# Weighted source one-hots in one operation, one column of each pair on VectorE and the other on GpSimd

## The chip, the cores and the metric

The kernel runs on one core of one Trainium2 chip. The metric is the device time of one execution in microseconds (us). The engines have the profile's names: PE is TensorE (matmuls), PEld its weight loads, DVE is VectorE, ACT is ScalarE, POOL is GpSimd, SP is SyncE.

## The reference, cut to what matters

Two layers of a graph network with attention and feed-forward parts work on 1250 nodes with 512 features. Only the edges of the graph convolution bear on this case:

```python
def _L0_gnn_ref(x, edge_index, edge_attr, W, b):
    ...
    deg = jax.ops.segment_sum(ew, col_f, num_segments=n)
    dinv = jnp.where(deg > 0, jax.lax.rsqrt(deg), 0.0)
    norm = dinv[row_f] * ew * dinv[col_f]
    h = x @ W
    msg = h[row_f] * norm[:, None]
    out = jax.ops.segment_sum(msg, col_f, num_segments=n)
    return out + b
```

There are 21250 edges, sorted by destination, each with a source, a destination and a weight.

## The kernel before

The kernel doesn't gather rows. It builds the dense matrix `AT` (source by destination, 10 x 10 tiles of 128) from the edges, and both graph layers then multiply by it. The edges lie in `CH` = 170 columns of 128, two columns to a pair, `CP` = 85 pairs. A pair's destinations lie in a window of `WIN` = 20 nodes. For pair `g`, TensorE multiplies a left one-hot `Loh` (128 edges by the 128 values of the source's low bits, times the edge's weight) with a right one-hot `Roh` (128 edges by 200 keys, which are 10 source tiles by 20 places in the window). The weight is kept as two parts, `whl`, a rounded one and the rest, so each pair has two columns times two parts: four matmuls of 128x200, all added in one PSUM bank `pW[g % 2]`. VectorE then adds the bank to the window of `AT`.

Who makes what for a pair, before the change:

- VectorE (`onehots`, L1327): two plain one-hots of the source, 128x128, into `onehot`; then the right one-hot of column 1 (L1329). It reports `oh_src` and `oh_dve`.
- GpSimd (L1000): one product of 128x512 that takes the two plain one-hots times the two weight parts into `Loh`. It waits for `oh_src` and reports `oh_pool`.
- ScalarE (L564, L566): the right one-hot of column 0, in two steps. It reports `oh_act`.
- TensorE (`adj`, L1989): waits for `oh_dve`, `oh_act`, `oh_pool` and, from the third pair on, for `a_acc`, the addition two pairs back. It reports `a_mm`.
- VectorE (`pairs_upto`, L1358): waits for `a_mm`, adds the bank to `AT`, and goes on with the one-hots three pairs further on.

`Loh` has `SLOTS` = 4 slots and `Roh` `RSLOTS` = 3, and `slot_free` is the wait for a slot: VectorE and ScalarE begin pair `g` when TensorE has done pair `g` - 3.

The pairs are woven into the products of the layer. A product (`product`, L2005) multiplies a tile of 128 nodes by one of the four weight matrices, in four blocks of three matmuls of 128x512. A fixed table (`pairs_by`, with `ADJ0` = 28 and `ADJ1` = 132) puts the 85 pairs behind the blocks 28 to 132, so that most blocks are followed by a pair. Between these come `kv` (L2034, twelve small matmuls) and the transposes of the next tile (L1976). For each tile VectorE also has `k_elu`, `xt_lo`, `v_lo` and `q_elu`, one operation of 128x512 each, and GpSimd has `k_lo` (L985, writes `khl`) once for 12 or 13 pairs. Every engine has one queue in the order in which the code is written.

Five operations of GpSimd elsewhere in the program serve as prices below: L1131 (a multiplication and an addition, both with a pointer, that is one value for each partition), L1115 (a multiplication and an addition of constants), L1117 and L1110 (a lone compare with a constant), and L1159 (a lone multiplication by a constant). Two of VectorE differ in a pointer: L1506 has one, L1862 a constant in its place.

When the pairs are done, VectorE reduces `AT` to the degrees (L1425), which TensorE's further work needs. SyncE loads `raw` after the last pair into the region that `onehot` shares.

Of the kernel before, what the change touches and what calls it, by code (L numbers as in the profile page):

```python
# [21 lines left out]
F32 = mybir.dt.float32  # L22
F32R = mybir.dt.float32r
I32 = mybir.dt.int32
ALU = mybir.AluOpType
# [3 lines left out]
P = 128  # L29
# [18 lines left out]
SLOTS = 4  # L48
ZERO_POOL, ZERO_DVE, ZERO_ACT = ((0, 1), (5, 6, 7)), (2, 3, 4), (8, 9)
RSLOTS = 3  # L50
# [52 lines left out]
def build(nc, a, out):  # L103
    ctx = ExitStack()
    with ctx:
# [24 lines left out]
        def region(name, *groups):  # L130
# [3 lines left out]
            for group in groups:  # L134
                used = 0
                with ExitStack() as r:
# [28 lines left out]
        srclo, key, whl, iota_src, iota_key = (RE[n] for n in ("srclo", "key", "whl", "iota_src", "iota_key"))  # L165
# [25 lines left out]
        R1 = region("hold_raw",  # L191
                    [("erow", [P, 3, 2, P], I32), ("frow", [P, 4, 2, P], F32)],

                    [("edge", [P, 3, CH]), ("egap", [P, 2 * D - 3 * CH]), ("away", [P, 2, T * WIN]), ("eq", [P, D])],
                    [("onehot", [P, SLOTS, 2, P], F32R)],
                    [("raw", [P, KC, D], F32)],
                    [("xb", [P, 2, D]), ("brow", [P, 2, D])],
                    [("vraw", [P, D]), ("b2", [P, 2, D], F32R)])
        erow, frow, edge, raw, xb, brow = (R1[n] for n in ("erow", "frow", "edge", "raw", "xb", "brow"))
        away, eq, onehot_ = R1["away"], R1["eq"], R1["onehot"]  # L200
        vraw, b2 = (R1[n] for n in ("vraw", "b2"))

        R2 = region("hold_weights",
# [35 lines left out]
        khl, vhl, Loh, Roh, ATs, Wv, qx, shl = (R3[n] for n in ("khl", "vhl", "Loh", "Roh", "ATs", "Wv", "qx", "shl"))  # L239
# [74 lines left out]
        S = {}  # L314
# [56 lines left out]

            return 8 * min(t, LAG) + 16 * max(0, t - LAG) + 4 * k

        def slot_free(eng, g):

            if g >= RSLOTS:
                eng.wait_ge(S["a_mm"], g - RSLOTS + 1)

        def evicted(w, t):

# [577 lines left out]
        def _(pool):  # L958
# [35 lines left out]

            pool.wait_ge(S["e_dve"], 1)
            for g in range(CP):
                pool.wait_ge(S["oh_src"], g + 1)
                w = whl[:, 2 * g:2 * g + 2, :].bitcast(F32).rearrange("p c (k n) -> p c k n", n=1).broadcast_to([P, 2, 2, P])
                o = onehot_[:, g % SLOTS].bitcast(F32).rearrange("p c (k n) -> p c k n", k=1).broadcast_to([P, 2, 2, P])
                pool.tensor_tensor(Loh[:, g % SLOTS], o, w, ALU.mult).then_inc(S["oh_pool"], 1)  # L1000
                for t in range(LAG, T):
                    if g == min(CP - 1, pairs_by(block_of(t, 2)) + 2):
                        k_lo(t)
# [22 lines left out]
            k = [0]  # L1026
# [66 lines left out]
            n = t1 - t0  # L1093
# [109 lines left out]
        def _(v):  # L1203
# [119 lines left out]

            def onehots(g):
                slot_free(v, g)
                for c in range(2):
                    ins = v.tensor_scalar(onehot_[:, g % SLOTS, c, :], iota_src[:], srclo[:, 2 * g + c:2 * g + c + 1], None, ALU.is_equal)  # L1327
                ins.then_inc(S["oh_src"], 1)
                v.tensor_scalar(Roh[:, g % RSLOTS, 1, :], iota_key[:], key[:, 2 * g + 1:2 * g + 2], None,  # L1329
                                ALU.is_equal).then_inc(S["oh_dve"], 1)  # L1330
# [635 lines left out]
        def _(pe):  # L1966
# [14 lines left out]
            def adj(g):  # L1981
                pe.wait_ge(S["oh_dve"], g + 1)
                pe.wait_ge(S["oh_act"], g + 1)
                pe.wait_ge(S["oh_pool"], g + 1)
                if g >= 2:
                    pe.wait_ge(S["a_acc"], g - 1)
                for c in range(2):
                    for part in range(2):
                        ins = pe.matmul(pW[g % 2][:, 0:T * WIN], Loh[:, g % SLOTS, c, part, :], Roh[:, g % RSLOTS, c, :],  # L1989
                                        start=(c + part == 0), stop=(c + part == 2))  # L1990
                ins.then_inc(S["a_mm"], 1)
# [612 lines left out]
```

## Time and profile before

| | |
|---|---|
| Median of 3 executions | 609.44 us (607.0 to 612.33) |
| The profiled execution | 611.55 us |
| Its span in the profile | 609.8 us |
| Busy: PE / PEld | 566.8 us (93%) / 457.4 us (75%) |
| Busy: DVE / ACT / POOL | 470.9 us (77%) / 331.7 us (54%) / 257.7 us (42%) |
| The stage with the pairs | 45.14 to 187.66 us |

The span is the time between the first and the last record of the profile; the 1.75 us between it and the execution's own time lie around it. Busy times are the union of an engine's records. TensorE's matmuls are pipelined and their ends are modelled, so a start to the next start says more there than a duration. The stage runs from the transposes behind the count of outside edges to the end of the last pair's matmuls.

### The profile page before, as it was taken

To read this page: it belongs to the slowest core of one execution; us is meant where nothing else is said; L and a number is where in the kernel's file an instruction comes from. 1 tells how busy PE (TensorE), PEld (TensorE's weight loads), DVE (VectorE), ACT (ScalarE), POOL (GpSimd) and SP (SyncE) were. 2 spreads that over 40 slices of the span, in tenths; PEclk is the share of its full clock that TensorE was granted. 3 is DMA by queue.
4 is the path that set the end of the run, shared out by engine and by line. 5 is a ranking of instruction groups with operands and counts; after the bars stand their busy time and mean duration, and the time that the engine had idled before them with its cause. 6 is when DMAs were issued, how large, how long until landed. Compare 5 with 4: busy or idle time off the path is not lost.

```text
span 609.8 us, 8679 instructions
## 1 busy us (share of the span) xinstructions
PE 566.8 (93%) x2933; PEld 457.4 (75%) x2933; DVE 470.9 (77%) x1043; ACT 331.7 (54%) x620; POOL 257.7 (42%) x290
## 2 busy tenths in 40 slices
PE   2998989988999999999999989999999999998977
PEld 2776877776887787888886757788878878687867
DVE  7679988979999688667988786778676556478865
ACT  7767868767775562213135656545456773423172
POOL 3647767667778515544833880005011221031020
PEclk9999989999999999999999999999999998899969
DMA  9300000000002021013113010000002000020004
GB/s 321 139 2 0 2 1 2 1 1 2 1 1 70 2 69 35 18 34 81 31 43 105 2 69 1 0 1 2 0 13 76 0 1 2 12 76 0 1 18 152
DMA packets 15046, 21.11 MB, mean 35 GB/s; under 512 B 3261, under 2 KB 6001, under 8 KB 15003
## 3 DMA queue, kind: packets, MB, share of 16 engines
q1 hardware_dynamic: 13674, 17.94, 9.2%
q10 hardware_dynamic: 1328, 2.62, 1.2%
q8 instruction: 24, 0.39, 0.3%
q14 instruction: 20, 0.16, 0.1%
HBM read 18.00 MB, written 2.56 MB: 34 GB/s over the span
## 4 chain that ended last, share of the span: by engine, by line
PE 62%; DVE 22%; ACT 7%; issue 5%; POOL 2%; DVEq 1%; ACTq 0%; POOLq 0%
PE p L2154 8%; PE p L1989 4%; PE pQ L2274 4%; PE p L2274 4%; PE pQ L2005 3%; DVE onehot L1327 3%; PE p L2410 2%; PE pH L2166 2%; PE pH L2005 2%; DVE p L1425 2%; PE p L2239 2%; PE pQ L2166 2%; PE pKV L2239 2%; POOL Loh L1000 2%; PE p L2005 2%
## 5 line engine op out<-in xcount | busy, mean ns | idle before, releaser
L1000 POOL TENSOR_TENSOR Loh<-onehot,whl 128x512 fp32r<-128x512 f32 x85 | 89.5, 1053 | 48.3 <-DVE onehot L1327 48.3
L1327 DVE TENSOR_SCALAR onehot<-iota_src,srclo 128x128 fp32r<-128x128 f32 x170 | 74.7, 479 | 0.7 <-DVE flagint L1339 0.7
L1989 PEld LDWEIGHTS p<-Roh,Loh 128*128 128x128 f32 x340 | 48.4, 192 | 31.1 <-issue 27.0
L2154 PE MATMUL p<-G,ATs 128*128 128x512 f32 x300 | 70.5, 391 | 0.0
L2154 PEld LDWEIGHTS p<-G,ATs 128*128 128x128 f32 x300 | 55.9, 188 | 11.6 <-issue 0.2
L1989 PE MATMUL p<-Roh,Loh 128*128 128x200 f32 x340 | 53.7, 281 | 11.3 <-POOL Loh L1000 4.8
L564 ACT ACTIVATE away<-iota_key,key 128x200 f32<-128x200 f32 x85 | 38.7, 456 | 24.4 <-PE p L1989 24.4
L2005 PE MATMUL pQ<-wsl,xT 128*128 128x512 f32 x168 | 48.4, 418 | 2.4 <-DVE xT L1241 2.4
L2005 PE MATMUL pH<-wsl,xT 128*128 128x512 f32 x168 | 46.4, 404 | 0.0
L1358 DVE TENSOR_TENSOR AT<-AT,p 128x200 f32 x85 | 30.1, 354 | 14.0 <-PE p L1989 8.8
L566 ACT ACTIVATE Roh<-away,onesf 128x200 fp32r<-128x200 f32 x85 | 39.4, 463 | 2.8
L1173 POOL TENSOR_TENSOR xT<-xn,xT 128x512 fp32r<-128x512 f32 x10 | 12.9, 1292 | 63.6 <-ACT xT L809 60.7
L1018 POOL TENSOR_TENSOR ATs<-AT,ATs 128x1280 fp32r<-128x1280 f32 x10 | 29.9, 2992 | 18.6 <-ACT ATs L624 18.3
L2005 PEld LDWEIGHTS pQ<-wsl,xT 128*128 128x128 f32 x168 | 30.6, 199 | 8.0 <-DVE xT L1241 3.2
L663 ACT ACTIVATE xT<-pT 128x512 fp32r<-128x512 f32 x10 | 6.0, 598 | 53.2 <-PE pT L2141 53.2
L2005 PE MATMUL p<-wsl,xT 128*128 128x512 f32 x120 | 33.2, 399 | 0.0
L2005 PEld LDWEIGHTS pH<-wsl,xT 128*128 128x128 f32 x168 | 29.7, 192 | 4.4
L2274 PE MATMUL p<-Wk,xT 128*128 128x512 f32 x120 | 30.1, 398 | 0.9 <-ACT rt L770 0.9
L2274 PE MATMUL pQ<-Wq,xT 128*128 128x512 f32 x120 | 29.9, 397 | 0.7 <-DVE xT L1668 0.5
L1329 DVE TENSOR_SCALAR Roh<-iota_key,key 128x200 fp32r<-128x200 f32 x85 | 26.6, 313 | 0.0
L1198 POOL TENSOR_SCALAR nodes<-nodes,small,nmr 128x512 f32<-128x512 f32 x10 | 8.0, 811 | 43.2 <-DVE sn L1881 43.2
L2274 PEld LDWEIGHTS pQ<-Wq,xT 128*128 128x128 f32 x120 | 21.9, 188 | 5.4 <-DVE xT L1668 0.6
(648 smaller groups left out, 1432.2 us busy)
## 6 DMA issues: line engine op xcount, KB each, us to landing
xb<-in_x SPq DMA_DIRECT2D x9, 256.0 KB, 2.6
out<-nodes SPq DMA_DIRECT2D x9, 256.0 KB
wraw<-in_L_mix_w_qkv ACTq DMA_DIRECT2D x2, 1024.0 KB, 7.5
raw<-in_L_mix_w_qkv SPq DMA_DIRECT2D x2, 1024.0 KB, 5.0
nodes<-in_x SPq DMA_DIRECT2D x1, 1024.0 KB, 9.0
wraw<-in_L_mix_w_qkv SPq DMA_DIRECT2D x1, 1024.0 KB, 11.3
wraw<-in_L_gnn_W SPq DMA_DIRECT2D x1, 1024.0 KB, 13.5
raw<-in_L_mix_w_out SPq DMA_DIRECT2D x1, 1024.0 KB, 5.3
```

The lines of the kernel that those rows point to most:

```text
L564: act.activation(away[:, g % 2, :], iota_key[:], ACT.Abs, bias=key[:, 2 * g:2 * g + 1], scale=-1.0).then_inc(S["oh_y"], 1)
L566: act.activation(Roh[:, g % RSLOTS, 0, :], away[:, g % 2, :], ACT.Relu, bias=onesf[:, 0:1], scale=-1.0).then_inc(S["oh_act"], 1)
L1000: pool.tensor_tensor(Loh[:, g % SLOTS], o, w, ALU.mult).then_inc(S["oh_pool"], 1)
L1018: pool.tensor_tensor(ATs[:, t % 2, 1], AT[:, :, t * P:(t + 1) * P], ATs[:, t % 2, 0].bitcast(F32), ALU.subtract).then_inc(S["ats_lo"], 1)
L1327: ins = v.tensor_scalar(onehot_[:, g % SLOTS, c, :], iota_src[:], srclo[:, 2 * g + c:2 * g + c + 1], None, ALU.is_equal)
L1329: v.tensor_scalar(Roh[:, g % RSLOTS, 1, :], iota_key[:], key[:, 2 * g + 1:2 * g + 2], None, ALU.is_equal).then_inc(S["oh_dve"], 1)
L1358: v.tensor_tensor(win, win, pW[g % 2][:, 0:T * WIN].rearrange("p (s w) -> p s w", s=T), ALU.add)\
L1989: ins = pe.matmul(pW[g % 2][:, 0:T * WIN], Loh[:, g % SLOTS, c, part, :], Roh[:, g % RSLOTS, c, :], start=(c + part == 0), stop=(c + part ...
L2005: ins = pe.matmul(bank[:, :], xT[:, t % XR, x, c, :], wsl[:, w, y, c, :], start=(c == 0 and n == 0), stop=(c == KC - 1 and n == 2))
L2154: ins = pe.matmul(pG[u][:, :], ATs[:, u, x, s_, :], G[:, y, s_, :], start=(s_ + n == 0), stop=(s_ == T - 1 and n == 2))
L2166: ins = pe.matmul(pM[u][:, :], xT[:, QT[u], x, c, :], WO[:, y, c, :], start=(c + n == 0), stop=(c == KC - 1 and n == 2))
L2274: ins = pe.matmul(o, xT[:, QT[u], x, c, :], w[:, y, c, :], start=(c + n == 0), stop=(c == KC - 1 and n == 2))
```

## The change

Each left one-hot is now made with its weight in it, by one `tensor_scalar` with two operations: compare `iota_src` with the source, multiply by the weight's part. VectorE makes the two parts of column 0, GpSimd the two parts of column 1, both straight into `Loh`. The buffer `onehot` is gone. GpSimd no longer waits for VectorE; it waits for its slot by itself, at the depth of `SLOTS` = 4. TensorE waits for `oh_src` too, besides `oh_pool`.

```diff
-        def slot_free(eng, g):
-
-            if g >= RSLOTS:
-                eng.wait_ge(S["a_mm"], g - RSLOTS + 1)
+        def slot_free(eng, g, slots=RSLOTS):
+
+            if g >= slots:
+                eng.wait_ge(S["a_mm"], g - slots + 1)
+
+        def weighted(eng, g, c, part):
+
+            col = slice(2 * g + c, 2 * g + c + 1)
+            return eng.tensor_scalar(Loh[:, g % SLOTS, c, part, :], iota_src[:], srclo[:, col], whl[:, col, part].bitcast(F32), ALU.is_equal, ALU.mult)
...
             pool.wait_ge(S["e_dve"], 1)
             for g in range(CP):
-                pool.wait_ge(S["oh_src"], g + 1)
-                w = whl[:, 2 * g:2 * g + 2, :].bitcast(F32).rearrange("p c (k n) -> p c k n", n=1).broadcast_to([P, 2, 2, P])
-                o = onehot_[:, g % SLOTS].bitcast(F32).rearrange("p c (k n) -> p c k n", k=1).broadcast_to([P, 2, 2, P])
-                pool.tensor_tensor(Loh[:, g % SLOTS], o, w, ALU.mult).then_inc(S["oh_pool"], 1)
+                slot_free(pool, g, SLOTS)
+                for part in range(2):
+                    ins = weighted(pool, g, 1, part)
+                ins.then_inc(S["oh_pool"], 1)
...
             def onehots(g):
                 slot_free(v, g)
-                for c in range(2):
-                    ins = v.tensor_scalar(onehot_[:, g % SLOTS, c, :], iota_src[:], srclo[:, 2 * g + c:2 * g + c + 1], None, ALU.is_equal)
+                for part in range(2):
+                    ins = weighted(v, g, 0, part)
                 ins.then_inc(S["oh_src"], 1)
...
             def adj(g):
                 pe.wait_ge(S["oh_dve"], g + 1)
                 pe.wait_ge(S["oh_act"], g + 1)
+                pe.wait_ge(S["oh_src"], g + 1)
                 pe.wait_ge(S["oh_pool"], g + 1)
```

In GpSimd's queue the start of the pairs reads before, from the last of the splits of the weights on (`wsl`) through the first `khl`:

```order
L980 TENSOR_TENSOR wsl<-wraw,wsl 128x512 x3
L1000 TENSOR_TENSOR Loh<-onehot,whl 128x512 [waits oh_src,e_dve]
L1000 TENSOR_TENSOR Loh<-onehot,whl 128x512 [waits oh_src] x5
L985 TENSOR_TENSOR khl<-rt,khl 128x512 [waits k_hi]
L1000 TENSOR_TENSOR Loh<-onehot,whl 128x512 [waits oh_src] x13
```

and now:

```order
L984 TENSOR_TENSOR wsl<-wraw,wsl 128x512 x3
L381 TENSOR_SCALAR Loh<-iota_src,srclo,whl 128x128 [waits e_dve]
L381 TENSOR_SCALAR Loh<-iota_src,srclo,whl 128x128 x7
L381 TENSOR_SCALAR Loh<-iota_src,srclo,whl 128x128 [waits a_mm]
L381 TENSOR_SCALAR Loh<-iota_src,srclo,whl 128x128
L381 TENSOR_SCALAR Loh<-iota_src,srclo,whl 128x128 [waits a_mm]
L381 TENSOR_SCALAR Loh<-iota_src,srclo,whl 128x128
L989 TENSOR_TENSOR khl<-rt,khl 128x512 [waits k_hi]
```

The first four pairs (eight operations) wait for nothing but the edges' weights and keys, and from the fifth on each pair waits for TensorE's count of done pairs in place of VectorE's one-hots; `khl` stands behind the sixth pair in both.

In TensorE's queue a block, its pair and the next block read before:

```order
L2005 MATMUL pQ<-wsl,xT 128x512 x2
L1989 MATMUL p<-Roh,Loh 128x200 [waits oh_pool,a_acc,oh_act,oh_dve]
L1989 MATMUL p<-Roh,Loh 128x200 x3
L2005 MATMUL pQ<-wsl,xT 128x512 [waits w_lo]
L2005 MATMUL pQ<-wsl,xT 128x512 x2
```

and now:

```order
L2010 MATMUL pQ<-wsl,xT 128x512 x2
L1994 MATMUL p<-Roh,Loh 128x200 [waits oh_pool,oh_src,a_acc,oh_act,oh_dve]
L1994 MATMUL p<-Roh,Loh 128x200 x3
L2010 MATMUL pQ<-wsl,xT 128x512 [waits w_lo]
L2010 MATMUL pQ<-wsl,xT 128x512 x2
```

Nothing has moved there but the one wait that is added to the pair's first matmul.

## Rows read from the trace of the kernel before

**Rows 1.** Windows: span, busy us and instructions of PE, PEld, DVE, ACT, POOL; PEclk; DMA
```profile
45.14:187.66 142.52, 131.22 (x749) 105.23 (x750) 128.06 (x365) 104.25 (x223) 98.68 (x93) 0.99 0.00 1
65.00:70.00 5.00, 5.00 (x33) 4.45 (x33) 4.49 (x14) 4.50 (x10) 3.67 (x4) 1.00 0.01 2
120.00:125.00 5.00, 4.24 (x24) 3.14 (x23) 5.00 (x13) 3.87 (x9) 4.03 (x5) 1.00 0.00 0
```

**Rows 2.** PE in order of time, 61 to 68 us: start us, us, operation
```profile
61.64 1.47 PE L2034 MATMUL pKV<-vhl,khl 128*128 128x130 f32 x12
62.95 0.91 PE L2005 MATMUL pH<-wsl,xT 128*128 128x512 f32 x3
...
66.41 0.87 PE L2005 MATMUL pH<-wsl,xT 128*128 128x512 f32 x3
67.12 0.59 PE L1989 MATMUL p<-Roh,Loh 128*128 128x200 f32 x4
67.55 0.60 PE L1976 MATMUL pT<-ident,xn 128*128 128x128 f32 x4
67.91 0.48 PE L2005 MATMUL p<-wsl,xT 128*128 128x512 f32 x1
```

**Rows 3.** Waits of PE in the stage: us in total, times, longest us
```profile
PE p L1989 <- POOL Loh L1000: 4.8, 11, 0.9
PE p L1989 <- DVE AT L1358: 4.1, 5, 1.7
```

**Rows 4.** DVE, then POOL and PE in order of time, 117 to 121 us, DVE at 137
```profile
117.33 0.47 DVE L1327 TENSOR_SCALAR onehot<-iota_src,srclo 128x128 fp32r<-128x128 f32 x2
117.72 0.31 DVE L1329 TENSOR_SCALAR Roh<-iota_key,key 128x200 fp32r<-128x200 f32 x1
117.95 0.35 DVE L1358 TENSOR_TENSOR AT<-AT,p 128x200 f32 x1
118.22 0.98 DVE L1327 TENSOR_SCALAR onehot<-iota_src,srclo 128x128 fp32r<-128x128 f32 x2
...
119.63 2.04 DVE L1327 TENSOR_SCALAR onehot<-iota_src,srclo 128x128 fp32r<-128x128 f32 x2
...
117.88 1.05 POOL L1000 TENSOR_TENSOR Loh<-onehot,whl 128x512 fp32r<-128x512 f32 x1 [1.04 <-DVE onehot L1327]
119.29 1.05 POOL L1000 TENSOR_TENSOR Loh<-onehot,whl 128x512 fp32r<-128x512 f32 x1 [0.36 <-DVE onehot L1327]
120.30 1.29 POOL L985 TENSOR_TENSOR khl<-rt,khl 128x512 fp32r<-128x512 f32 x1
...
119.21 0.67 PE L1989 MATMUL p<-Roh,Loh 128*128 128x200 f32 x4 [0.28 <-POOL Loh L1000]
...
137.12 0.36 DVE L1358 TENSOR_TENSOR AT<-AT,p 128x200 f32 x1 [3.38 <-issue]
```

**Rows 5.** The page's costliest groups: busy us, mean ns of one | idle before
```profile
L1327 DVE TENSOR_SCALAR onehot<-iota_src,srclo 128x128 fp32r<-128x128 f32 x170 | 74.7, 479 | 0.7 <-DVE flagint L1339 0.7
```

**Rows 6.** Groups by line of POOL's TENSOR_SCALAR: busy us, mean ns | idle before
```profile
L1131 POOL TENSOR_SCALAR nodes<-nodes,small,nmr 128x512 f32<-128x512 f32 x10 | 7.5, 765 | 0.1
L1115 POOL TENSOR_SCALAR first<-first 128x16 f32<-128x16 f32 x1 | 0.2, 205 | 3.2 <-DVE first L1682 3.2
L1117 POOL TENSOR_SCALAR XB<-first 128x16 f32<-128x16 f32 x1 | 0.3, 252 | 0.1
L1110 POOL TENSOR_SCALAR XB<-XB 128x256 f32<-128x256 f32 x1 | 0.9, 857 | 0.1
L1159 POOL TENSOR_SCALAR pairq<-pairs 128x64 fp32r<-128x64 f32 x1 | 0.4, 408 | 0.0
```

**Rows 7.** Groups by line of DVE: one form with a pointer, one with a constant
```profile
L1506 DVE SCALAR_TENSOR_TENSOR nodes<-p,dinv,nodes 128x512 f32<-128x512 f32 x10 | 7.5, 751 | 0.9 <-PE p L2154 0.6
L1862 DVE SCALAR_TENSOR_TENSOR nodes<-p,nodes 128x512 f32<-128x512 f32 x10 | 6.8, 681 | 0.0
```

**Rows 8.** The chain that ended last, behind the last pair: start us, us
```profile
188.96 11.87 DVE p L1425
```

More of the change, by code:

```diff
@@ L194, in build @@
                     [("edge", [P, 3, CH]), ("egap", [P, 2 * D - 3 * CH]), ("away", [P, 2, T * WIN]), ("eq", [P, D])],
-                    [("onehot", [P, SLOTS, 2, P], F32R)],
                     [("raw", [P, KC, D], F32)],
@@ L199, in build @@
         erow, frow, edge, raw, xb, brow = (R1[n] for n in ("erow", "frow", "edge", "raw", "xb", "brow"))
-        away, eq, onehot_ = R1["away"], R1["eq"], R1["onehot"]
+        away, eq = R1["away"], R1["eq"]
         vraw, b2 = (R1[n] for n in ("vraw", "b2"))
```

## The prediction

> **What bounds the kernel now.** I read the stretches first, then TensorE's order of time at a good and a bad place, then the order of time of the engines that feed it, and last the waits. The change touches one stage: the 85 pairs run from 45.14 us, where TensorE has finished the count of outside edges, to 187.66 us, the end of the last pair. In that stage TensorE is busy for 131.22 of 142.52 us [rows 1], which looks like a full engine. It isn't. Between 65 and 70 us it issued 33 matmuls, between 120 and 125 us only 24, in both at a granted clock of 1.00 [rows 1]; its records stretch when it has to wait. The good place gives the price of everything on TensorE, start to start: a pair's four matmuls 67.12 to 67.55 = 0.43 us, a block of three products 66.41 to 67.12 = 0.71, the twelve of kv 61.64 to 62.95 = 1.31, the four transposes 67.55 to 67.91 = 0.36 [rows 2]. The stage holds 85 pairs, 104 blocks, six kv and six groups of transposes: 36.6 + 73.8 + 7.9 + 2.2 = 120.4 us. So TensorE loses 22 us to its feeders. Its plain waits (4.8 us on GpSimd's product, 4.1 on the addition to AT) show less than half of that [rows 3].
>
> The feeders run in a ring. At 117 to 122 us the reader sees two one-hots on VectorE, 0.47 us for both when GpSimd is idle, 0.98 us when GpSimd's product is in the air: the second pair starts at 118.22 and ends at 119.20, which is 0.27 after GpSimd's 117.88 + 1.05 = 118.93. Then GpSimd starts at 119.29, 0.09 later, and holds VectorE's next pair in turn. Product to product, 117.88 to 119.29, is 1.41 us [rows 4]. TensorE in the same place could take a pair every 0.43 + 0.71 = 1.14 us, so this ring sets the pace wherever each block has its pair. The total says that this is the rule: the one-hots kept VectorE busy for 74.7 us, where 85 pairs at 0.47 would be 40, so some 35 us of that is being held [rows 4, 5]. With khl in GpSimd's queue VectorE's two one-hots ran 2.04 us in place of 0.98 (119.63) [rows 4], so the ring takes 1.06 more, seven times. 85 × 1.41 + 7 × 1.06 = 127 us of the 142.5; the other 15 are the first pairs, stalls of VectorE like the 3.38 us with no releaser shown at 137 us [rows 4], and places in which TensorE itself was late.
>
> **The change on GpSimd.** 85 products of 1.05 us go [rows 4], and 170 compares with a multiplication, 128x128, come. No row shows that operation. Its nearest rows are in two families [rows 6]. Multiplication and addition with two pointers, 128x512, took 765 ns, and two such with constants on 128x16 took 205: 0.190 us and 1.12 ns for each element, so 0.33 us for 128. A lone compare took 252 ns on 16 elements and 857 on 256: 0.212 us and 2.52 ns, so 0.53 us; a lone multiplication, 408 ns on 64, is on that dear line or above it. So what is cheap is the joined multiplication and addition, not two operations as such. If each operation paid the dear rate by itself it would be 0.212 + 2 × 128 × 0.00252 = 0.86 us. I take 0.56, the compare's line, which is the nearest operation, with 0.03 for the second; bounds 0.33 and 0.86. For a pair: 1.12 us, from 0.66 to 1.72, against 1.05 before, but without VectorE ahead of it. GpSimd now waits for the pair four back on TensorE, and may do the first four while it used to wait at the start.
>
> **The change on VectorE.** Two plain one-hots a pair become two with a second pointer. A pointer cost 751 - 681 = 70 ns on a comparable form [rows 7]; between 0 and 0.07 each, so 0 to 0.14 a pair. I take 0.05 for both, since one pointer is already being read. VectorE's own work in a pair is 0.27 (addition to the next one-hot, 117.95 to 118.22) + 0.39 (117.33 to 117.72) + 0.23 (117.72 to 117.95) = 0.89 us [rows 4], now 0.94 to 1.03.
>
> **How they share.** VectorE's compares stand still while GpSimd works. But the two held one-hots ended 0.27 us after GpSimd, of which the second took its usual 0.19, so the first needed only 0.08 more. And when GpSimd went from the product straight to khl (119.29 + 1.05, then 120.30), one of VectorE's two got through between and only the second was held; khl took 1.29 all the same [rows 4]. So one compare slips in at each handover, at no cost to GpSimd. Let p be GpSimd's operation. I count from the end of a pair's last feeder on VectorE, Roh. TensorE's pair follows and is reported about 1.0 us later (an estimate: 0.43 of matmuls, and what lay between GpSimd's end at 118.93 and the start at 119.21 of TensorE's pair, twice [rows 2, 4]); there GpSimd starts its two operations, for the pair four on. Those of the cycle before ended at 1.0 + 2p - C. VectorE has one one-hot through at their handover, ends the other 0.08 after their end, and Roh with 0.28 behind it; that is the end of the next Roh, so C = 1.0 + 2p - C + 0.36, or C = 0.68 + p. At p = 0.56 that is 1.24 us a pair, against 1.41. It can't be under GpSimd's own 2p + 0.1 (1.22) or VectorE's 0.94.
>
> The feeders then need 85 × 1.24 + 7 × 1.06 = 113 us, under TensorE's 120.4. TensorE becomes the bound on average, though not in stretches with a pair behind every block (1.24 against 1.14), where a lead of three pairs covers some of it. What stays: VectorE's stalls with no releaser (3.38 at 137; this one left TensorE short by 1.2), the first pairs (some 2 us), k_elu and xt_lo of 1.2 us in a row on VectorE. I put these at 11 to 13 us: 120.4 + 12 = 132.5, so the stage gives back **10 us**.
>
> The Trainium skill (SBUF — State Buffer, Who interferes with whom) says that the pair of ports is locked for the whole instruction, whoever comes first, and the other fully blocks. That speaks against this change. By the recorded durations it would make 0.47 + 0.31 + 1.05 = 1.83 us a pair before, and 0.78 + 1.12 = 1.90 after, a loss of 6 us in 85. The trace agrees that the loser is held, but not with the sum: the ring took 1.41.
>
> **Edits with one answer.** The onehot buffer isn't needed; no transfer waits for it. TensorE's new wait for oh_src stands in a queue that ran into a pair 0.43 us behind the last block with four waits already, so I cost it at nothing; if each showed, 85 × 0.05 = 4 us. The seven khl on GpSimd come two to three pairs earlier in the order of time, and may wait for ScalarE; behind them only pairs four ahead are queued. After the stage the path is VectorE's reduction of 11.9 us [rows 8], which starts at the last addition, and nothing earlier holds it. So all that the stage gives reaches the end.
>
> **The sum.** 611.55 us (span 609.8, 1.75 around it) - 10 = 601.5 for that execution, which lay 2.1 over the median of 609.44. Against the median: 599.5, said as 600.
>
> **Rivals.**
> (1) GpSimd on the cheap line, p = 0.33. C falls to 1.01, TensorE is the bound nearly throughout and the stage takes 120.4 + 6 us: 16 us gained, 594. For it: the two-pointer row of 765 ns. Against: every compare in the trace is dear. The Trainium skill (GPSIMD Engine Reference, Performance pitfalls for Q7 kernels) gives a compare-and-select body 1.03 to 2.03 cycles an element, which at its 1.2 GHz is an estimate of 0.9 to 1.7 ns and would bring this rival's time; the compare's 2.52 ns doesn't agree [rows 6].
> (2) **Slower: GpSimd becomes the bound.** With both operations at the dear rate, p = 0.86 and C = 2p + 0.1 = 1.82: 85 × 1.82 + 7.4 = 162 us, and 5 for the start, 167 against 142.5: 634. It decides above the point where 85 × (2p + 0.1) eats what the ring had, 127 - 7.4 = 120: p = 0.66. Half way, at 0.76, C = 1.62 and the time is 618 to 625. For it: the lone multiplication at 408 ns on 64 elements shows how dear one step is. Against: one operation or two need not double the loop.
> (3) The compares slip in less than I think, and VectorE is held for all of GpSimd's 1.12: C = 0.27 + 1.12 = 1.39 and more with what used to hide under the product (0.6 us of evictions four times in 12 pairs). Then 606 to 612, no change.
> (4) The change may not do all it says: without its fast form the one-hot on VectorE takes 0.07 us longer but isn't held. That ends near the forecast.
>
> **Chances.** Forecast (596 to 603): 0.40, case 4 in it. Rival 1: 0.18. Rival 3 with p near 0.66: 0.19. Rival 2: 0.23. Two executions of this kernel differ by up to 0.9% (607.0 to 612.33), so 1%, or 6 us, is what a measurement can tell from no change. Faster takes rival 1 and nearly all of the forecast: 0.57; within 1%: 0.20; slower: 0.23. The range runs from 592, under rival 1, to 630, where about half of rival 2 is in it; some 0.14 stay out.
>
> **What the profile after would show.** The 170 operations on GpSimd at 0.50 to 0.62 us; above 0.7, rival 2, with TensorE waiting for GpSimd in most pairs. VectorE's 170 weighted one-hots with a mean between 0.3 and 0.45 us, where it is 0.479 now [rows 5]. 30 or more matmuls in most 5 us of the stage. No wait of GpSimd for VectorE; its idle time now ends with TensorE's pairs. The last pair near 178 us, the reduction right behind it, and the rest of the program as long as before (422 us). Wrong would be an end of the stage outside 170 to 185, or a gain there that is lost again after it.

## The result and the profile after

| | before | after |
|---|---|---|
| Median (six executions each, same chip) | 607.1 us (605.62 to 612.33) | 620.01 us (618.63 to 621.53) |
| Profiled execution, its span | 611.55, 609.8 | 620.04, 618.3 |
| End of the last pair | 187.66 us | 196.73 us |
| Start of the reduction behind it | 188.96 us | 198.02 us |

The change made the kernel slower by 2.0%: the ratio is 1.0196, with a 95% interval from 1.016 to 1.0232. (This ratio and those below aren't quotients of the two medians.) The profiled executions differ by 8.5 us only, since the one of before lay 4.5 above this median (the last section shows where such 4 us come from). I read the page first: the busy times, the chain by engine, and the three groups that answer to [rows 5] and to GpSimd's new operation (busy us, mean ns | idle before).

```profile
span 618.3 us, 8765 instructions
...
PE 565.1 (91%) x2933; PEld 453.1 (73%) x2933; DVE 458.8 (74%) x1043; ACT 332.6 (54%) x620; POOL 314.3 (51%) x375
...
PE 50%; POOL 24%; DVE 17%; ACT 7%; issue 2%; ACTq 0%; DVEq 0%
...
L381 POOL TENSOR_SCALAR Loh<-iota_src,srclo,whl 128x128 fp32r<-128x128 f32 x170 | 145.9, 872 | 1.2 <-PE p L1994 1.2
...
L1362 DVE TENSOR_TENSOR AT<-AT,p 128x200 f32 x85 | 30.3, 356 | 35.6 <-PE p L1994 28.7
L381 DVE TENSOR_SCALAR Loh<-iota_src,srclo,whl 128x128 fp32r<-128x128 f32 x170 | 55.7, 380 | 0.7 <-DVE flagint L1343 0.7
```

One row settles what bounds the stage. GpSimd's 170 operations took 145.9 us with 1.2 us of idle time between them: the engine never had to wait for anybody. VectorE, which the old ring held, has lost that: its 170 compares take 55.7 us in place of 74.7 [rows 5], and it waits 28.7 us for TensorE before the addition. Before, GpSimd had 48.3 us of idle time in front of its products, all of it waiting for VectorE:

```profile
L1000 POOL TENSOR_TENSOR Loh<-onehot,whl 128x512 fp32r<-128x512 f32 x85 | 89.5, 1053 | 48.3 <-DVE onehot L1327 48.3
```

The windows say the same; they are the whole stage, the 5 us that [rows 1] shows of before, and the rest of the program (span, busy us and instructions of PE, PEld, DVE, ACT, POOL; PEclk; DMA).

```profile
45.00:196.73 151.73, 131.73 (x749) 103.12 (x750) 115.65 (x365) 105.09 (x223) 150.11 (x172) 1.00 0.00 1
120.00:125.00 5.00, 4.25 (x23) 3.01 (x22) 4.53 (x12) 3.62 (x8) 5.00 (x6) 1.00 0.00 0
196.73:618.30 421.57, 401.63 (x2037) 324.96 (x2036) 309.54 (x602) 194.50 (x351) 135.94 (x167) 0.98 0.11 33
```

GpSimd is busy for 150.11 of 151.73 us, where it was 98.68 of 142.52 [rows 1]. TensorE issues 23 matmuls from 120 to 125 us, one less than before. The rest takes 421.6 us against 422.1, so the end of the stage, 9.1 us later, accounts for all of the 8.5 us that the profiled execution lost. In order of time, the stretch that [rows 4] shows of before reads (start us, us, operation, idle before):

```profile
116.81 6.13 POOL L381 TENSOR_SCALAR Loh<-iota_src,srclo,whl 128x128 fp32r<-128x128 f32 x7
...
117.85 0.67 PE L1994 MATMUL p<-Roh,Loh 128*128 128x200 f32 x4 [0.40 <-ACT Roh L570]
...
118.93 0.60 DVE L381 TENSOR_SCALAR Loh<-iota_src,srclo,whl 128x128 fp32r<-128x128 f32 x2
119.44 0.32 DVE L1333 TENSOR_SCALAR Roh<-iota_key,key 128x200 fp32r<-128x200 f32 x1
119.66 0.67 PE L1994 MATMUL p<-Roh,Loh 128*128 128x200 f32 x4 [0.45 <-DVE Loh L381]
...
121.37 0.66 PE L1994 MATMUL p<-Roh,Loh 128*128 128x200 f32 x4 [0.33 <-DVE Loh L381]
...
122.91 1.32 POOL L989 TENSOR_TENSOR khl<-rt,khl 128x512 fp32r<-128x512 f32 x1
123.00 1.34 DVE L1333 TENSOR_SCALAR Roh<-iota_key,key 128x200 fp32r<-128x200 f32 x1
123.28 0.60 PE L1994 MATMUL p<-Roh,Loh 128*128 128x200 f32 x4
...
126.20 0.67 PE L1994 MATMUL p<-Roh,Loh 128*128 128x200 f32 x4 [1.62 <-POOL Loh L381]
```

GpSimd's seven operations in a row take 6.13 us, 0.876 each, and TensorE's pairs start 1.71 to 1.81 us apart (117.85, 119.66, 121.37), where the ring had 1.41 [rows 4]. Around khl a pair starts 2.92 us after the one ahead of it (123.28 to 126.20). TensorE's waits, 8.9 us for two producers before [rows 3], name VectorE's `Loh` for about as much time as GpSimd's (us in total, times, longest), because both halves have the same name and end near each other; the idle time of GpSimd, not these names, tells which one is late.

```profile
PE p L1994 <- DVE Loh L381: 6.2, 12, 1.4
PE p L1994 <- POOL Loh L381: 6.1, 9, 1.6
...
PE p L1994 <- DVE AT L1362: 2.6, 4, 1.2
```

The chain behind the end of the stage is GpSimd's line almost alone (start us, us):

```profile
179.29 9.48 POOL Loh L381 x12
...
189.47 3.54 POOL Loh L381 x4
193.00 1.25 POOL khl L989
194.25 1.56 POOL Loh L381 x2
195.81 0.24 issue
196.05 0.68 PE p L1994 x4
...
198.02 11.85 DVE p L1429
```

The reduction begins 198.02 - 188.96 = 9.1 us later [rows 8].

### The profile page after: what moved, and what is told of

Same layout as the page of the kernel before. It is cut to its first block, busy times and chain, and to the rows that moved or that the text cites. A ratio compares the mean times of both kernels' runs of the same rounds, so it can differ in the third digit from the quotient of the medians.

```text
span 618.3 us, 8765 instructions
## 1 busy us (share of the span) xinstructions
PE 565.1 (91%) x2933; PEld 453.1 (73%) x2933; DVE 458.8 (74%) x1043; ACT 332.6 (54%) x620; POOL 314.3 (51%) x375
## 4 chain that ended last, share of the span: by engine, by line
PE 50%; POOL 24%; DVE 17%; ACT 7%; issue 2%; ACTq 0%; DVEq 0%
POOL Loh L381 22%; PE p L2159 8%; PE p L2279 4%; PE pQ L2279 4%; PE p L2415 2%; PE pH L2171 2%; DVE p L1429 2%; PE p L2244 2%; PE pQ L2171 2%; PE pKV L2244 2%; POOL khl L989 1%; PE pH L2478 1%; PE pQ L2010 1%; PE pKV L2443 1%; PE pH L2415 1%
## 5 line engine op out<-in xcount | busy, mean ns | idle before, releaser
L381 POOL TENSOR_SCALAR Loh<-iota_src,srclo,whl 128x128 fp32r<-128x128 f32 x170 | 145.9, 872 | 1.2 <-PE p L1994 1.2
L1994 PEld LDWEIGHTS p<-Roh,Loh 128*128 128x128 f32 x340 | 46.7, 190 | 42.5 <-issue 27.9
L2159 PEld LDWEIGHTS p<-G,ATs 128*128 128x128 f32 x300 | 55.9, 188 | 11.6 <-issue 0.2
L1362 DVE TENSOR_TENSOR AT<-AT,p 128x200 f32 x85 | 30.3, 356 | 35.6 <-PE p L1994 28.7
L381 DVE TENSOR_SCALAR Loh<-iota_src,srclo,whl 128x128 fp32r<-128x128 f32 x170 | 55.7, 380 | 0.7 <-DVE flagint L1343 0.7
L1333 DVE TENSOR_SCALAR Roh<-iota_key,key 128x200 fp32r<-128x200 f32 x85 | 33.1, 389 | 0.0
L1168 POOL CAST Wv<-raw 128x512 fp32r<-128x512 f32 x4 | 3.3, 862 | 52.0 <-DVE nmr L1240 52.0
```

The source lines that it names most:

```text
L381: return eng.tensor_scalar(Loh[:, g % SLOTS, c, part, :], iota_src[:], srclo[:, col], whl[:, col, part].bitcast(F32), ALU.is_equal, ALU.mult)
L1362: v.tensor_tensor(win, win, pW[g % 2][:, 0:T * WIN].rearrange("p (s w) -> p s w", s=T), ALU.add)\
L2159: ins = pe.matmul(pG[u][:, :], ATs[:, u, x, s_, :], G[:, y, s_, :], start=(s_ + n == 0), stop=(s_ == T - 1 and n == 2))
```

## The experiments

Theory: GpSimd's operation costs what rival 2 said, because both operations and both pointers are paid for, and everything else is as forecast. Rival theories: the new wait of TensorE, VectorE's dearer compares, or the two engines holding each other. Ratios are to the kernel before on the same chip, with 95% intervals; its medians there were 610.0 to 610.2.

**Three cheaper operations on GpSimd.** First a lone compare, without the weight.

```diff
-                    ins = weighted(pool, g, 1, part)
+                    ins = pool.tensor_scalar(Loh[:, g % SLOTS, 1, part, :], iota_src[:], srclo[:, slice(2 * g + 1, 2 * g + 2)], None, ALU.is_equal)
```

> The changed kernel, but GpSimd's two operations of each pair are a lone compare with the source's pointer; the multiplication by the weight is left out there, for column 1. Theory A (the number of operations sets GpSimd's price: 0.79 us for two, each about 2.3 ns an element over 0.2 us): an operation takes 0.50 to 0.55 us, GpSimd is no longer the bound, and the kernel takes 596 to 604 us, as my forecast had it for 0.56. Rival B (the compare with pointers is dear in itself, and the second operation free): 0.75 us or more each, 612 to 620. Rival C (what is long is being held by VectorE at the ports): still above 0.7 us while VectorE works, and 612 or more.

Then the same two pointers with a multiplication and an addition.

```diff
-                    ins = weighted(pool, g, 1, part)
+                    ins = pool.tensor_scalar(Loh[:, g % SLOTS, 1, part, :], iota_src[:], srclo[:, slice(2 * g + 1, 2 * g + 2)], whl[:, slice(2 * g + 1, 2 * g + 2), part].bitcast(F32), ALU.mult, ALU.add)
```

> The changed kernel, but GpSimd's two operations of each pair are a multiplication and an addition with the same two pointers in place of the compare and the multiplication, so that column 1 holds other numbers. Theory A: 0.33 us each, as the trace's line for this form says; GpSimd is free half of the time, TensorE or VectorE set the pace and the kernel takes 592 to 598 us, as my rival 1 had it. Rival B: as A here. Rival C (held at the ports): 0.45 us or more each with a large spread, 598 to 606. If the kernel takes as long as before (604 to 610) with 0.33 us, then the price of GpSimd was not all of it, and the forecast's picture of what else bounds the stage is wrong.

And, on another chip, the compare with a constant factor.

```diff
-                    ins = weighted(pool, g, 1, part)
+                    ins = pool.tensor_scalar(Loh[:, g % SLOTS, 1, part, :], iota_src[:], srclo[:, slice(2 * g + 1, 2 * g + 2)], 0.5, ALU.is_equal, ALU.mult)
```

> The changed kernel, with GpSimd multiplying by the constant 0.5 in place of the weight's pointer (column 1 then has a wrong weight). It splits what the second operation costs on GpSimd: 0.60 us was the lone compare with one pointer, 0.79 the compare and the multiplication with two. If the second pointer is dear, this operation takes 0.60 to 0.65 us and the kernel 600 to 604; if the second operation is, 0.70 to 0.79 us and 608 to 618.

The instances of `Loh` on GpSimd (ns min/median/max, first and last start us), in the kernel after:

```profile
L381 POOL TENSOR_SCALAR Loh<-iota_src,srclo,whl x170: 783/820/1224, 40.0 to 195.0; 128x128 fp32r<-128x128 f32 x170
```

With the lone compare:

```profile
L1003 POOL TENSOR_SCALAR Loh<-iota_src,srclo x170: 594/602/856, 39.5 to 177.6; 128x128 fp32r<-128x128 f32 x170
```

With the multiplication and addition:

```profile
L1003 POOL TENSOR_SCALAR Loh<-iota_src,srclo,whl x170: 443/484/885, 39.9 to 174.5; 128x128 fp32r<-128x128 f32 x170
```

With the constant factor:

```profile
L1003 POOL TENSOR_SCALAR Loh<-iota_src,srclo x170: 708/717/1210, 39.1 to 180.7; 128x128 fp32r<-128x128 f32 x170
```

By the lowest and the medians, the lone compare costs 0.60 us and a factor adds 0.11. A pointer in its place adds 0.07 by the lowest, which makes 0.78; the median of the kernel after, 0.82, holds more than the operation itself, as the run without column 0 shows below. The means of the three runs are 616, 498 and 786 ns. The joined multiplication and addition costs 0.44 to 0.48. Medians: 600.62 us for the lone compare, ratio 0.9866 (0.983 to 0.9901); 600.84 for the multiplication and addition, 0.9867 (0.9833 to 0.9901); 603.53 for the constant factor, from two executions, 0.9878 (0.9835 to 0.992). All three leave the weight out of column 1 or put another number in its place; only their times matter here. The whole change with another operation on this one line is a gain, so neither the new wait nor VectorE's part made the loss. What the cheapest operation adds to the lone compare is not settled: its reduction starts at 178.89 us against 182.04, 3.1 earlier, but the medians are 0.2 apart.

**The new wait alone**, in the kernel before.

```diff
                 pe.wait_ge(S["oh_act"], g + 1)
+                pe.wait_ge(S["oh_src"], g + 1)
                 pe.wait_ge(S["oh_pool"], g + 1)
```

> The kernel before with nothing but the added wait of TensorE for VectorE's count of source one-hots. I cost it at nothing, with 4 us if it showed each time: 607 to 612, ratio 1.000 within 0.3%. A rival that puts the loss on the fifth wait in TensorE's queue would want 615 or more.

609.14 us, ratio 0.9968 (0.9933 to 1.0002): no cost of the wait shows.

**Does VectorE lengthen GpSimd's operation?** The kernel after, with column 0 made for the first four pairs alone, so that beside GpSimd VectorE compares only for `Roh`, once a pair. (TensorE then multiplies by what stands in the slots, and the later use of the count `oh_src` goes by `SLOTS` too.)

```diff
-                for part in range(2):
-                    ins = weighted(v, g, 0, part)
-                ins.then_inc(S["oh_src"], 1)
+                if g < SLOTS:
+                    for part in range(2):
+                        ins = weighted(v, g, 0, part)
+                    ins.then_inc(S["oh_src"], 1)
...
-                pe.wait_ge(S["oh_src"], g + 1)
+                pe.wait_ge(S["oh_src"], min(g + 1, SLOTS))
```

> The changed kernel, but VectorE makes its two one-hots of column 0 for the first four pairs alone; after that TensorE multiplies by what stands in the slots, so the sums are of other edges. It takes 162 of VectorE's compares out of GpSimd's way. GpSimd's operation took 0.79 us before VectorE had begun and 0.87 in the mean after. If VectorE's compares lengthen it, the mean falls to 0.80 to 0.82 and the last pair ends 6 to 9 us earlier: 610 to 614 us, with GpSimd still the bound. If the longer ones have another cause (TensorE, ScalarE, the queue), 0.86 to 0.87 stays and the kernel takes 617 to 621.

The page's group for GpSimd's line here, and its instances (ns min/median/max, first and last start us):

```profile
L381 POOL TENSOR_SCALAR Loh<-iota_src,srclo,whl 128x128 fp32r<-128x128 f32 x170 | 134.4, 804 | 1.2 <-PE p L1995 1.2
...
L381 POOL TENSOR_SCALAR Loh<-iota_src,srclo,whl x170: 783/788/1194, 39.4 to 182.9; 128x128 fp32r<-128x128 f32 x170
```

609.98 us, ratio 1.0035 (0.9998 to 1.0072), and the reduction starts at 185.93, 12.1 earlier than after. GpSimd is as full as in the kernel after (1.2 us idle in both), so the difference is its own: 145.9 - 134.4 = 11.5 us. So the operation itself costs 0.79 (the median here), and VectorE's two compares beside each pair stretch its mean from 0.80 to 0.87.

The other way round there is hardly any effect. In the kernel after, two compares on VectorE take 0.60 us while GpSimd works (118.93 above). With all four on VectorE and no compare on GpSimd, two of them take as long (0.59 at 116.86 below, the last two of a pair), and the medians of one are 341 and 335 ns:

```diff
-                for part in range(2):
-                    ins = weighted(pool, g, 1, part)
-                ins.then_inc(S["oh_pool"], 1)
+                pool.engine_nop().then_inc(S["oh_pool"], 1)
...
-                for part in range(2):
-                    ins = weighted(v, g, 0, part)
+                for c in range(2):
+                    for part in range(2):
+                        ins = weighted(v, g, c, part)
```

> VectorE makes all four weighted one-hots of a pair; GpSimd only passes its count on. Theory A: VectorE needs 4 x 0.26 + 0.50 = 1.54 us a pair and 0.6 us for each of four evictions a tile, nothing holds it but the seven khl: 85 x 1.54 + 28 x 0.6 = 148 us for the stage, against 142.5 before and 151 in the changed kernel: 611 to 618 us. Rival C (ports): if VectorE's operations are slowed by GpSimd in the changed kernel, they show 0.33 us without exception here and the kernel is faster than 608.

VectorE in order of time there:

```profile
116.86 0.59 DVE L381 TENSOR_SCALAR Loh<-iota_src,srclo,whl 128x128 fp32r<-128x128 f32 x2
...
117.88 1.11 DVE L381 TENSOR_SCALAR Loh<-iota_src,srclo,whl 128x128 fp32r<-128x128 f32 x4
...
119.41 1.12 DVE L381 TENSOR_SCALAR Loh<-iota_src,srclo,whl 128x128 fp32r<-128x128 f32 x4
```

628.31 us, ratio 1.0301 (1.027 to 1.0333): VectorE is the bound, with its pairs 1.53 us apart (117.88 to 119.41) and no idle time.

**Is it the kind of GpSimd's operation that holds VectorE?** A product of two tensors comes back for column 1, 128x256, with one plain one-hot; column 0 stays on VectorE.

```diff
-                for part in range(2):
-                    ins = weighted(pool, g, 1, part)
-                ins.then_inc(S["oh_pool"], 1)
+                pool.wait_ge(S["oh_src"], g + 1)
...
+                pool.tensor_tensor(Loh[:, g % SLOTS, 1], o, w, ALU.mult).then_inc(S["oh_pool"], 1)
...
+                v.tensor_scalar(onehot_[:, g % SLOTS, :], iota_src[:], srclo[:, 2 * g + 1:2 * g + 2], None, ALU.is_equal).then_inc(S["oh_src"], 1)
                 for part in range(2):
-                    ins = weighted(v, g, 0, part)
-                ins.then_inc(S["oh_src"], 1)
+                    weighted(v, g, 0, part)
```

(`slot_free` on GpSimd and TensorE's wait for `oh_src` go as well.)

> VectorE makes the two weighted one-hots of column 0 and a plain one-hot of column 1, and GpSimd multiplies that one by the two parts of the weight, a product of 128x256 in the form of the kernel before. GpSimd's product should take 0.55 to 0.6 us (1.05 for 128x512). VectorE: 0.19 + 0.52 + 0.50 = 1.21 us a pair, and it is held by the product again. If being held by a product of two tensors is what made the ring before, the pace is 0.6 + 0.36 = 0.96 for the ring and VectorE's 1.21 plus up to 0.4 sets it: 604 to 612. If GpSimd's product no longer holds VectorE at the wrong moment, VectorE's 1.21 sets it: 598 to 604.

VectorE, then GpSimd, in order of time:

```profile
118.70 0.27 DVE L1331 TENSOR_SCALAR onehot<-iota_src,srclo 128x128 fp32r<-128x128 f32 x1
118.89 0.89 DVE L382 TENSOR_SCALAR Loh<-iota_src,srclo,whl 128x128 fp32r<-128x128 f32 x2
...
119.05 0.65 POOL L1005 TENSOR_TENSOR Loh<-onehot,whl 128x256 fp32r<-128x256 f32 x1 [0.86 <-DVE onehot L1331]
```

The same two compares take 0.89 us beside the product and 0.60 beside GpSimd's compares. They end at 119.78, 0.08 after the product. The time is 628.0 us, ratio 1.0276 (1.0211 to 1.0341), with a pair every 1.51 us: VectorE is held for 0.3 of each and is the bound.

**Other shares.** Three of a pair's four parts on VectorE, one on GpSimd; then that in every second pair; then in every third.

```diff
-                for part in range(2):
+                for part in range(g % 2, 2):
                     ins = weighted(pool, g, 1, part)
...
                     ins = weighted(v, g, 0, part)
+                if g % 2:
+                    ins = weighted(v, g, 1, 0)
```

(This is the second; the first has it for all `g`, the third for `g % 3 == 1`.)

> VectorE makes three of the four weighted one-hots of a pair (column 0 and the rounded part of column 1), GpSimd one. Theory A (GpSimd's price of 0.8 us an operation is the bound of the changed kernel): GpSimd needs 0.85 a pair, VectorE 3 x 0.26 + 0.50 = 1.28 and what it is held; the pace is 1.3 to 1.4 us, so 85 x 0.4 = 34 us less than now would be the feeders' gain, but TensorE's own 120 us of the stage stand before: 598 to 606 us. Rival C (ports): VectorE's three are held by GpSimd's one and by khl, 1.28 + 0.5 = 1.8 a pair: 618 or more.

> The split of the four weighted one-hots changes with the pair: even pairs as in the changed kernel (two on VectorE, two on GpSimd), odd pairs three on VectorE and one on GpSimd. If GpSimd's 0.80 to 0.86 us an operation was the only fault, GpSimd now needs 1.5 x 0.83 = 1.25 us a pair and VectorE 2.5 x 0.26 + 0.50 = 1.15: 85 x 1.25 + 9 = 115 us on GpSimd, 85 x 1.15 + 28 x 0.6 = 115 on VectorE, both under TensorE's 120, so 598 to 604 us, faster than both kernels. If instead the weighted compare on VectorE costs the gain wherever it stands (three of four on VectorE gave 611.8), 606 to 610.

> As the alternating split, but GpSimd gives one of its two one-hots away only in every third pair. GpSimd: 142 operations of 0.87 and the khl, 133 us; VectorE 0.045 us a pair less than in the alternating split, in which TensorE waited for VectorE (9.7 us) and GpSimd idled (17 us): 603 to 608 us. If it is slower than the alternating split (607.6), GpSimd bounds it again.

In all pairs: 611.8 us, ratio 1.0042 (1.0006 to 1.0078); GpSimd waits 54.4 us for TensorE, TensorE 13.7 us for VectorE's addition, so VectorE is the bound. In every second: 607.56, 0.9959 (0.9925 to 0.9992), GpSimd idle for 17.1 us. In every third: 603.52, 0.9929 (0.9889 to 0.9968), GpSimd idle for 2.3. In the profiled executions the reduction starts at 189.62, 185.49 and 182.87 us, so of these three the share with the least idle time on GpSimd has the shortest stage. (The 4 us between the last two medians are another matter: see the last section.)

**A cheaper form on VectorE.** One `scalar_tensor_tensor` makes both parts of a column, 128x256. First for both columns, GpSimd left out; then column 0 always, and column 1 in odd pairs, while GpSimd makes column 1 of the even ones as in the kernel after. The diff is the second's.

```diff
+        def column(eng, g, c):
+
+            w = whl[:, 2 * g + c, :].bitcast(F32).rearrange("p (k n) -> p k n", n=1).broadcast_to([P, 2, P])
+            i = iota_src[:].rearrange("p (k n) -> p k n", k=1).broadcast_to([P, 2, P])
+            return eng.scalar_tensor_tensor(Loh[:, g % SLOTS, c], i, srclo[:, 2 * g + c:2 * g + c + 1], w, ALU.is_equal, ALU.mult)
...
+                if g % 2:
+                    ins = pool.engine_nop()
+                else:
+                    for part in range(2):
+                        ins = weighted(pool, g, 1, part)
                 ins.then_inc(S["oh_pool"], 1)
...
+                ins = column(v, g, 0)
+                if g % 2:
+                    ins = column(v, g, 1)
```

> VectorE makes both columns, each with one operation over 256 elements (compare with the source, multiply by the two parts of the weight as a second tensor), and GpSimd has no part in the pairs. An estimate from the rows for 256 elements with two tensors (0.42 us) and for a pointer (0.07) is 0.49 a column, 0.40 start to start: 0.80 + 0.50 = 1.30 us a pair, and 28 evictions of 0.6: 128 us for VectorE, with its stalls 134: 600 to 608 us. If VectorE's time per pair is what sets a kernel without GpSimd, the four separate operations (1.54 a pair, 628 us) and this one differ by 85 x 0.24 = 20 us, so 608; if something else in VectorE's queue sets it, no more than 10 us better.

> Column 0 by one operation of VectorE over 256 elements, column 1 by GpSimd's two operations in even pairs and by one more of VectorE in odd pairs. GpSimd: 86 x 0.87 + 9 = 84 us, VectorE: 1.5 x 0.40 + 0.50 = 1.10 a pair, 85 x 1.10 + 17 + 6 = 117 us, both under TensorE's 120: 596 to 602 us if the engines' sums decide. An operation with two tensors in SBUF may be held by GpSimd where the compares of one tensor were not: then 0.5 us and more are lost in every even pair, and it takes 605 to 615.

The page's groups of the second:

```profile
L381 POOL TENSOR_SCALAR Loh<-iota_src,srclo,whl 128x128 fp32r<-128x128 f32 x86 | 83.0, 972 | 39.8 <-PE p L2004 39.7
...
L387 DVE SCALAR_TENSOR_TENSOR Loh<-iota_src,srclo,whl 128x256 fp32r<-128x256 f32 x127 | 62.2, 516 | 0.7 <-DVE flagint L1353 0.7
```

And its chain, behind the last pair:

```profile
180.90 11.86 DVE p L1439
```

The first took 612.08 us, ratio 1.0067 (1.0035 to 1.0099), 16 less than with four compares. Two such operations in a row took 0.87 us (at 119.54 us of the second kernel's trace), four compares 1.11 (117.88 above). The second took 599.84 us, ratio 0.9897 (0.9837 to 0.9958). It beats both kernels, and its reduction starts 8.1 us before that of the kernel before [rows 8]. GpSimd's operation is at its longest here, 0.97 on average, but it has 39.8 us of idle time to pay for that. VectorE isn't held by it: its operation of 128x256 takes 516 ns on average, and 513 in the first of the two, in which GpSimd has no part.

**Where the expectations missed.** Wherever VectorE had more than its two compares, I had set the time too low: 628 us for at most 618 (all four), 628 for at most 612 (half product), 612 for at most 606 (three of four), 607.6 for at most 604 (every second pair), 612 for at most 608 (columns on VectorE alone). In the first, VectorE's group and the window are:

```profile
L381 DVE TENSOR_SCALAR Loh<-iota_src,srclo,whl 128x128 fp32r<-128x128 f32 x340 | 101.0, 357 | 0.7 <-DVE flagint L1342 0.7
...
45.00:205.00 160.00, 134.57 (x749) 106.18 (x748) 153.63 (x536) 104.98 (x223) 9.71 (x8) 0.98 0.00 1
```

VectorE's time for a pair was as reckoned (1.53 for 1.54). My 148 us for the stage left out what the seven khl hold, an estimate of 101.0 - 85 × 1.11 = 7 us, and 6 us in which VectorE was idle. In the other direction, I had 608 to 618 us for a second operation that is dear on GpSimd; with the constant factor it was (0.71 us), and the kernel took 603.5.

## Why the prediction was wrong

**The step that failed** is the price of GpSimd's operation: "I take 0.56, the compare's line, which is the nearest operation, with 0.03 for the second; bounds 0.33 and 0.86". It measured 0.872 on average. The compare's line was nearly right (0.53 against 0.60 for the lone compare, which has a pointer where the rows had constants). The 0.03 was wrong: factor and pointer cost 0.19 (0.79 - 0.60), and with VectorE's compares beside it the mean came to 0.872, 0.08 more. I had taken how cheap the joined multiplication and addition is for a sign that a second operation costs little; it costs little there only. The Trainium skill (GPSIMD Engine Reference, Performance pitfalls for Q7 kernels) speaks of 1.03 to 2.03 cycles an element for a compare and a selection, in kernels written for the engine; the prediction made that an estimate of 0.9 to 1.7 ns. With the 0.212 us of the prediction for the start, this operation took (0.783 - 0.212) / 128 = 4.5 ns an element even at its shortest, so the trace doesn't agree for this built-in operation.

**Rival 2** is what happened to the kernel: GpSimd became the bound. That its price (0.86) met the mean (0.872) is in part luck. It let the second operation cost as much as the first, 0.32 us; factor and pointer cost 0.19. The rest of the 0.87 was a lone compare 0.06 above the line and VectorE's lengthening of 0.08, and it had neither. Its 634 us were 14 too many. By its own terms: it had 2p + 0.1 a pair, 154.7 us, but GpSimd's operations ran end to end, 145.9. It had 5 us more for the start; GpSimd instead began at 40.04, 5.1 ahead of the stage, since it makes four pairs before it waits for any, and TensorE ended 0.9 behind its last operation: 5 + 5.1 - 0.9 = 9.2. Against these, khl took 9.0 for 7.4, and 1.2 us were idle. 8.8 + 9.2 - 1.6 - 1.2 = 15, which is 167 - 152.

**The point from which it decides** was too low as well. I had p = 0.66, from the ring's 120 us alone; rival 2's own sum, with 7.4 for khl and 5 for the start, meets the old 142.5 us at (142.5 - 12.4 - 8.5) / 170 = 0.72. A full GpSimd pays 1.7 us of the stage for each 0.01 us of p: from the run without column 0 to the kernel after, 0.804 to 0.872, 0.068 makes 11.6, and the reduction moved by 12.1. Without column 0 it starts 3.0 before that of [rows 8], so by the stage the old time is met near a mean of p = 0.82, an estimate. The run with the constant factor lies on the same line: a mean of 0.786, 2.2 us idle, the reduction at 183.60, 5.4 before that of [rows 8], and a gain. The median without column 0 is no better than that of before (ratio 1.0035), so at 0.80 what is shown is a stage 3.0 us shorter, but no gain in the time. Between that and the loss of 2.0% stands the lengthening by VectorE, which no term of mine had on GpSimd's side.

**The way they share** was told the wrong way round. "VectorE's compares stand still while GpSimd works", and one slipping in at each handover, holds for products of two tensors: the run with the half product shows it, and `Roh` beside khl took 1.34 us (123.00) for its usual 0.32. GpSimd's compares don't hold VectorE, 0.60 us against 0.59 with no compare on GpSimd; it is they that are stretched. The rule of the Trainium skill that I weighed (SBUF — State Buffer, Who interferes with whom), that whoever comes second is fully blocked for the whole instruction, agrees with the product and khl, and doesn't with this operation. Why the kinds differ, no run here shows.

**The size of the gain where GpSimd is not the bound** was near, though a little large. At p = 0.60 I had C = 1.28 and 10 us. The run with the lone compare ended its stage 188.96 - 182.04 = 6.9 us earlier, the one with p = 0.48 10.1 us. Of the stalls of VectorE with no releaser that the forecast let stay, the one of 3.38 us stands in front of the addition of pair 51 = 3 × 17, before which the code loads 17 window positions into registers, and a stall of this kind, 2.6 to 4.0 us at the longest, stayed in every version. Rival 1's 16 us were not there: TensorE then waits for VectorE's addition, 8.6 and 7.5 us in total, where rival 1 left 6 us for all that stays. Its price of 0.33 us for the joined multiplication and addition was low too: 0.44 at the least.

**Rival 3** fell: VectorE isn't held by GpSimd's compares. **Rival 4** is open. Its price fits: a weighted compare takes at least 328 ns where the plain one took 272, and the two of a pair 0.51 us to the start of the next operation (118.93 to 119.44) where it was 0.39, so 0.06 each for its 0.07 (I had 0.05 for both). But that compare is held by a product of two tensors (0.89 us), so that GpSimd's compares leave it alone isn't shown to come from its form, and whether it lost its fast form no run here shows. **Right** were the costs set at nothing (the wait, and khl's place, since GpSimd never waits for it), that GpSimd's idle time ends with TensorE, and that the end of the stage passes to the end of the program whole (421.6 us against 422.1). The sign to look for, above 0.7 us on GpSimd's line, was the right one, and the end of the stage at 196.7 fell outside the 170 to 185 named.

## What to carry to other kernels

Price an operation on GpSimd by a row with the same pair of operations and the same pointers, or measure it alone in one run: here the compare with a weight cost 0.79 us where its near relatives cost 0.48 and 0.60. A step that is moved to break a wait between two engines needs slack where it lands; work out at which duration that engine is full, and what its neighbour adds. When such a change loses, try other shares before undoing it: here the same idea with half of GpSimd's part moved to a cheaper form on VectorE gained 1.0%.

## What the runs showed of the hardware

The rest of the program isn't the same in every execution. The clock granted over the whole execution sorts the kernel before into two groups: on one of the chips, ten executions at 0.988 to 0.990 took 605.63 to 608.39 us, fifteen at 0.979 to 0.983 took 609.77 to 611.63. Two traces show one such place. In the profiled execution of before, TensorE's 48 matmuls of `pKV` from `ZT` took 9.96 us, and the granted clock was 0.82, 0.50 and 0.66 in the three stretches of 5 us from 510 on; in the run with the lone compare the same 48 took 6.36 us, at 1.00. The windows of before, then of the lone compare:

```profile
515.00:520.00 5.00, 5.00 (x25) 5.00 (x25) 0.63 (x1) 0.00 (x0) 0.00 (x0) 0.50 0.01 3
```

```profile
504.00:509.00 5.00, 4.86 (x38) 4.44 (x39) 4.61 (x8) 1.18 (x4) 0.00 (x0) 1.00 0.01 3
```

A granted clock of 0.50 is the lower level, 1.2 GHz. In both, TensorE had just waited 0.8 us for `rt` and 0.5 us for `ZT`, with transposes between; why the clock fell in one and not in the other isn't settled. (Both have a further stretch at 0.50 near their end, from 585 on before and at 575 with the lone compare.) It bears on the gains above: less than 602 us was reached only at 0.987 or more. At a like clock, the lone compare stands at 600.6 against 605.65 on its chip (0.989 and 0.991) and at 604.5 against 611.2 (0.980 both), a gain of 5 to 7 us, which is its stage's 6.9 and not the 9.4 of the medians. The best version has 603.93 at 0.980 and before 610.5 to 611.2 there: 7 us, with 8.1 in the stage. The shares of every second and every third pair come out even: at 0.979 to 0.982, every second pair has 607.25 to 607.59 and every third 606.61 to 607.58, though the medians are 4 us apart, so which of them is faster isn't shown beyond the 2.6 us between their stages.

The loss of the change needs the same care. Its medians are 12.9 us apart, its profiled executions 8.5, the ends of its stage 9.1. The profiled execution of after has the slow stretch too (the 48 matmuls took 9.08 us), so the stage's 9.1 is the figure to keep; the executions of after were granted 0.972 to 0.986, and for the six of before no clock is recorded.
